# The input projection of an attention layer as three f32r products, with weight slices read from device memory and the split work placed anew

## What is computed

```
def _L0_cond_ref(x, mask, Wq, Wo):        # NH = 8 heads, dk = 64
    xt = jnp.transpose(x, (0, 2, 1))
    q = xt @ Wq.T
    qh = q.reshape(B, T, NH, dk).transpose(0, 2, 1, 3)
    scores = scale * jnp.einsum('bhqd,bhkd->bhqk', qh, qh)
    logits = (scores * cmask + (1.0 - cmask) * NEG) * rmask
    attn = jax.nn.softmax(logits, axis=-1)
    ctx = jnp.einsum('bhqk,bhkd->bhqd', attn, qh)
    ctx = ctx.transpose(0, 2, 1, 3).reshape(B, T, D)
    out = ctx @ Wo.T
    return jnp.transpose(out, (0, 2, 1))

x = x + _L0_cond_ref(x, cond_2048, L0_cond_Wq, L0_cond_Wo)
x = x + _L1_cond_ref(x, cond_2048[:, None, :], L1_cond_b)   # causal conv over 16 sequences, plus a bias
```

## Time and profile before

| | |
|---|---|
| median of 3 runs | 4114.28 us (4113.2 to 4120.28) |
| the profiled execution | 4113.86 us |
| its span | 4112.1 us |
| mean granted TensorE clock | 0.99 |
| TensorE busy | 3982.2 us, 97% of the span |
| ScalarE, GpSimd, VectorE busy | 2768.7, 2683.2 and 2395.2 us |
| loads and stores of device memory | 44 GB/s over the span |

### The profile page before, as it was taken

How to read it: one execution, slowest core, us unless ns; L and a number is a source line. 1 busy time by engine, 2 the same in 40 slices (tenths; PEclk the granted TensorE clock), 3 DMA queues, 4 the chain that set the end, 5 groups by cost and what they waited for, 6 DMA issues and landing times. The chain is left out here.

```text
span 4112.1 us, 58673 instructions
## 1 busy us (share of the span) xinstructions
PE 3982.2 (97%) x19200; PEld 2608.8 (63%) x19200; DVE 2395.2 (58%) x2263; ACT 2768.7 (67%) x3848; POOL 2683.2 (65%) x1105
## 2 busy tenths in 40 slices
PE   7999999999999999999999999999999999999799
PEld 4666666666666666665666666666666666666598
DVE  4665555556465555656555565656556555656676
ACT  4775767667576766757676675767667676767465
POOL 4775767767576776757676675767668576767200
PEclk8999999999999999999999999999999999999899
DMA  4433444343444434344343434434443443443587
GB/s 113 103 93 88 100 106 113 92 109 88 97 102 95 118 93 103 93 97 102 91 118 94 103 93 103 104 88 113 98 106 85 103 107 90 110 103 71 159 291 264
DMA packets 308556, 452.16 MB, mean 110 GB/s; under 512 B 155043, under 2 KB 223267, under 8 KB 308134
## 3 DMA queue, kind: packets, MB, share of 16 engines
q1 hardware_dynamic: 308262, 448.18, 43.5%
HBM read 112.28 MB, written 67.11 MB: 44 GB/s over the span
## 5 line engine op out<-in xcount | busy, mean ns | idle before, releaser
L759 POOL TENSOR_TENSOR plo<-p,phi 128x1024 fp32r<-128x1024 f32 x1024 | 2535.8, 2486 | 1146.8 <-ACT phi L675 1143.5
L810 DVE TENSOR_REDUCE mrow<-misc 128x1 f32<-128x1024 f32 x1024 | 1200.9, 1214 | 826.2 <-PE misc L502 826.0
L673 ACT ACTIVATE p<-sc 128x512 f32<-128x512 f32 x2048 | 1108.6, 593 | 753.8 <-PE sc L544 616.6
L675 ACT ACTIVATE phi<-p 128x1024 fp32r<-128x1024 f32 x1024 | 1086.2, 1061 | 32.6
L543 PE MATMUL sc<-quer,keys 128*128 128x512 f32 x2048 | 879.7, 430 | 21.3 <-issue 17.8
L556 PE MATMUL pv<-phi,val 128*96 128x512 f32 x2048 | 850.9, 415 | 18.0 <-issue 18.0
L544 PE MATMUL sc<-quer,keys 96*128 96x512 f32 x2048 | 811.8, 396 | 0.0
L558 PE MATMUL pv<-phi,val 128*64 128x512 f32 x2048 | 808.9, 395 | 0.0
L562 PE MATMUL pv<-plo,val 128*96 128x512 f32 x2048 | 641.8, 395 | 0.9 <-POOL plo L759 0.9
L556 PEld LDWEIGHTS pv<-phi,val 128*96 128x96 f32 x2048 | 332.3, 162 | 335.4 <-issue 172.2
L543 PEld LDWEIGHTS sc<-quer,keys 128*128 128x128 f32 x2048 | 387.8, 189 | 169.5 <-issue 57.8
(11 more groups left out here) (80 smaller groups left out, 3480.4 us busy)
## 6 DMA issues: line engine op xcount, KB each, us to landing
keys<-hi SPq DMA_DIRECT2D x256, 256.0 KB, 3.1
quer<-mhi SPq DMA_DIRECT2D x256, 256.0 KB, 4.9
keys<-lo SPq DMA_DIRECT2D x128, 256.0 KB, 5.9
quer<-mlo SPq DMA_DIRECT2D x128, 256.0 KB, 3.8
xo<-x SPq DMA_DIRECT2D x64, 512.0 KB, 4.3
x<-xo SPq DMA_DIRECT2D x64, 512.0 KB, 4.8
xin<-x SPq DMA_DIRECT2D x16, 2048.0 KB, 13.8
out<-stage SPq DMA_DIRECT2D x64, 512.0 KB, 6.3
```

What stands on the lines that cost most here:

```text
L673: act.activation(p32[:, t % NP32, half(h)], sc[:, h, :], ACT.Exp, scale=SCALE).then_inc(s_p32, 1)
L675: act.activation(phi[:, t % NPHI, :], p32[:, t % NP32, :], ACT.Copy).then_inc(s_phi, 1)
L759: pool.tensor_tensor(plo[:, t % NPLO, :], p32[:, t % NP32, :], phi[:, t % NPHI, :].bitcast(F32), ALU.subtract).then_inc(s_plo, 1)
L810: reduced = dve.tensor_reduce(mrow[:, q:q + 1], misc[:, k, :], AX.X, ALU.max)
```

## The change

The input projection becomes three f32r products as well. x and both weights are split into a high part rounded to f32r and the remainder: xh and xl, wqh and wql, woh and wol. The weights are split once, at the start, stored to device memory (`keep`), and read back in slices of 512 KB: one for each pair (`wqs`, `load_wq`), one for each quarter of the output (`wos`, `load_wo`). x is loaded to `x32` in four parts at pair 2, head 0, behind the transfer of the row of maxima; ScalarE makes xh of it and VectorE and GpSimd two parts of xl each, in head 1 of pair 2. `mlo` gives up its buffer and is made in `lo`, once `lo` has been moved. The tables of maxima, stages, reciprocals, normalisation and of the split of the context are new.

```diff
+HI_AT = {0: 0, 2: 1, 3: 2, 4: 3}
+LO_POOL = {3: 1, 6: 3}
+LO_DVE = {1: [0], 5: [2]}
-MAX_AT = {0: [0, 1], 1: [2, 3], 3: [4, 5], 4: [6, 7]}
+MAX_AT = {0: [0, 1], 2: [2, 3], 3: [4, 5], 4: [6, 7]}
-REC_AT = {(0, 5): [0], (0, 6): [1], (0, 7): [2], (1, 0): [3], (1, 1): [4], (1, 2): [5], (1, 3): [6], (1, 4): [7]}
-NORM_AT = (1, 5)
+REC_AT = {(0, 5): [0, 1], (0, 6): [2, 3], (0, 7): [4, 5], (1, 5): [6], (1, 6): [7]}
+NORM_AT = (1, 7)
-STAGE_AT = {2: ["mhi", "lo"], 3: ["mlo"]}
-HIGH_AT = (1, 7)
-LOW_AT = (1, 7)
+STAGE_AT = {2: ["mhi"], 3: ["lo"], 6: ["mlo"]}
+HIGH_AT = (0, 0)
+LOW_AT = (0, 0)
...
@@ block.sync
+                if not (isinstance(b, int) and b == 0 and p == 0):
+                    if isinstance(b, int) and b == B - 1 and p == PAIRS - 1:
+                        sp.dma_start(wqs[:].bitcast(F32), wo_kept[2].rearrange("w p k e -> p w k e")).then_inc(s_wqs, 16)
+                    else:
+                        load_wq((p + 1) % PAIRS)
...
+            def keep(t, n, kept, done):
+                sp.wait_ge(done, n)
+                sp.dma_start(kept.rearrange("m p k e -> p k m e"),
+                             t.bitcast(F32).rearrange("p k (m e) -> p k m e", e=P)).then_inc(s_kept, 16)
...
             def store_xo(b, m, more=0):
                 sp.wait_ge(s_xo, b * 2 * DT + 2 * m + 2 + more)
+                if more:
+                    load_wo(3, 0)
+                elif not (isinstance(b, int) and b == B - 1):
+                    load_wo((m + 2) % DT, m % 2)
...
                 operands(0, 0)
+                keep(wqh, 2, wq_kept[:, 0], s_wqh)
+                keep(wql, 2, wq_kept[:, 1], s_wql)
+                keep(woh, 1, wo_kept[:, 0], s_wo_high)
+                keep(wol, 1, wo_kept[:, 1], s_wol)
                 operands2(0, 0, 0, None)
+                sp.wait_ge(s_kept, 64)
+                load_wq(1)
+                for m in range(2):
+                    load_wo(m, m)
                 sp.wait_ge(s_zero, 3)
                 rows(0, 0, 0)
...
                         if phase != "last" and (p, i) == (2, 1):
-                            load_x(b + 1, pair(b, 3) + 1)
+                            load_mask(b + 1, pair(b, 3) + 1)
...
                             rows(nb, np_, ni)
+                        if phase != "last" and (p, i) == (2, 0):
+                            for k in range(DT):
+                                load_x(b + 1, k)
...
@@ block.tensor
-                for k in range(DT):
-                    last = pe.matmul(out, wq[:, k, np_ * P:(np_ + 1) * P], xb[:, k, half(h)],
-                                     start=(k == 0), stop=(k == DT - 1))
+                elif h == 0:
+                    pe.wait_ge(s_wqs, 16 * pair(nb, np_))
+                if phase != "start" and h == 0 and np_ == 0:
+                    pe.wait_ge(s_xl, split_done(nb, 2, 2))
+                    pe.wait_ge(s_xl_pool, 2 * nb)
+                for n, (w, xs) in enumerate(((0, xh), (1, xh), (0, xl))):
+                    for k in range(DT):
+                        last = pe.matmul(out, wqs[:, w, k, :], xs[:, k, half(h)],
+                                         start=(n == 0 and k == 0), stop=(n == 2 and k == DT - 1))
...
@@ block.scalar
+            def input_high(b, k):
+                act.wait_ge(s_xk[k], 16 * b)
+                act.activation(xh[:, k, :], x32[:, k, :], ACT.Copy).then_inc(s_xh, 1)
...
+                            if phase != "last" and (p, i) == (2, 1) and t in HI_AT:
+                                input_high(b + 1, HI_AT[t])
-                            if (i, t) == HIGH_AT and not (phase == "first" and p == 0):
-                                context_high(*before(b, p))
+                            if (i, t) == HIGH_AT and not (phase == "first" and p < 2):
+                                context_high(*before(*before(b, p)))
...
@@ block.gpsimd
+            def input_low(b, k):
+                pool.wait_ge(s_xh, split_done(b, DT, k + 1))
+                pool.tensor_tensor(xl[:, k, :], x32[:, k, :], xh[:, k, :].bitcast(F32), ALU.subtract).then_inc(s_xl_pool, 1)
...
@@ block.vector
                     dve.wait_ge(s_lo, pair(b, p) + 1)
-                    dve.tensor_tensor(mlo[:], lo[:].bitcast(F32), mask[:], ALU.mult).then_inc(s_masked, 1)
+                    for i in range(2):
+                        dve.wait_ge(s_kq[i], 64 * (pair(b, p) + 1))
+                    dve.tensor_tensor(lo[:], lo[:].bitcast(F32), mask[:], ALU.mult).then_inc(s_masked, 1)
...
+            def input_low(b, k):
+                dve.wait_ge(s_xh, split_done(b, DT, k + 1))
+                dve.tensor_tensor(xl[:, k, :], x32[:, k, :], xh[:, k, :].bitcast(F32), ALU.subtract).then_inc(s_xl, 1)
```

More of the change, by code:

```diff
@@ L373, in operands2 @@
                 move(keys2[0:DK, i, :], hi, i).then_inc(s_kq2[i], 16)
[L374 removed]
+                move(quer2[0:DK, i, :], lo, i).then_inc(s_kq2[i], 16)
             def context_rows(b, p, i):
@@ L525, in out_project @@
                     pe.wait_ge(s_ctl, PAIRS * (prev_b + 1))
-                cols = slice(m * P, (m + 1) * P)
-                for n, (w, c) in enumerate(((woh, cth), (wol, cth), (woh, ctl))):
+                ws = wqs if phase == "end" and m == 2 else wos[:, 0 if phase == "end" and m == 3 else m % 2]
+                if phase == "end" and m == 2 and h == 0:
+                    pe.wait_ge(s_wqs, 16 * PAIRS * B)
+                elif phase == "end" and m == 3 and h == 0:
+                    pe.wait_ge(s_wos[0], 16 * (2 * B))
+                elif h == 0:
+                    pe.wait_ge(s_wos[m % 2], 32 * prev_b + 16 * (m // 2) + 16)
+                for n, (w, c) in enumerate(((0, cth), (1, cth), (0, ctl))):
                     for k in range(PAIRS):
-                        last = pe.matmul(out, w[:, k, cols], c[:, k, half(h)],
+                        last = pe.matmul(out, ws[:, w, k, :], c[:, k, half(h)],
                                          start=(n == 0 and k == 0), stop=(n == 2 and k == PAIRS - 1))
@@ L775, in batch, with end @@
                             split(b, p, i, t, phase == "first" and p == 0 and i == 0)
-                            if (i, t) == LOW_AT and not (phase == "first" and p == 0):
-                                context_low(*before(b, p))
-            run(pool, start, batch, lambda: None)
+                            if phase != "last" and (p, i) == (2, 1) and t in LO_POOL:
+                                input_low(b + 1, LO_POOL[t])
+                            if (i, t) == LOW_AT and not (phase == "first" and p < 2):
+                                context_low(*before(*before(b, p)))
+            def end():
+                context_low(B - 1, PAIRS - 2)
+            run(pool, start, batch, end)
         @block.vector
@@ L880, in start @@
                 table_masks()
-                for parts in STAGE_AT.values():
-                    for part in parts:
-                        stage(0, 0, part)
+                dve.wait_ge(s_wqh, 1)
+                dve.tensor_tensor(wqs[:, 1], wq32[:, :, 0:P], wqs[:, 0].bitcast(F32), ALU.subtract).then_inc(s_wql, 1)
+                first_low(0)
+                first_low(1)
+                stage(0, 0, "mhi")
+                stage(0, 0, "lo")
+                weights_low()
+                stage(0, 0, "mlo")
                 do("start", 0, 0, "head", PHASES["start"]["head"], (0, 0, 0))
-                weights_low()
             def batch(phase, b):
@@ L900, in batch @@
                                     normalise(*before(b, p))
+                            if phase != "last" and (p, i) == (2, 1):
+                                for k in LO_DVE.get(t, []):
+                                    input_low(b + 1, k)
             def table_masks():
```

98 lines of the change are left out of this document (68 added, 30 removed).

## The result

| | before | after |
|---|---|---|
| median of 4 runs each, us | 4113.74 (4111.21 to 4120.28) | 4085.43 (4082.28 to 4090.08) |
| the profiled execution's span | 4112.1 | 4083.8 |
| mean granted TensorE clock | 0.990 | 0.988 |

The ratio is 0.9928, with a 95% interval of 0.9916 to 0.994: the change makes the kernel 28 us faster. 4132 was forecast, and slower was given 0.57.

The account below looks back on a forecast made before the run. TensorE, 97% busy, was taken as the bound. From 4113.9 us: -79 - 18 + 22 + 50 + 22 + 6 + 15 = +18, so 4132 us; own range 4120 to 4146, whole range 4070 to 4176.

Parts of the forecast that it names:

- lo and mlo: Pairs other than pair 2: late mlo delays the next head's maxima, costing 0.75 us twice a batch, +22 us.
- Only their cost moves: Head 0: moving two tiles of maxima from step 1 to step 2 only moves their cost, no saving.
- x remainders: Pair 2, head 1: GpSimd's load makes TensorE wait before pair 3's first projection; +3.35 us a batch, +50 us.
- rival B: Remainders of x cost TensorE nothing, waiting under 0.5 us at pair 3's first projection; 4082 us, chance 0.25.
- SP: Pair 1: SP's queue of transfers brings head 1's row of maxima late, +0.4 us a batch, +6 us.
- the projection: Input projection: twelve f32r matmuls take 2.80 us where four fp32 took 3.43, over 126 halves, -79 us.
- the cover of the copy: Step 2 of head 1: maxima cover the wait for ScalarE's copy, 2.91 us becomes 2.33, -18 us.
- pair 1: Output halves wait for banks of maxima (1.16, 0.8, 1.0 us), an old wait of 1.42 goes; +22 us.
- the start: First scores come at 52 to 60 us for 42.5, behind splits, stores and slices of weights; +14 us.
- `lo` comes first in the loop: Head 0, other pairs than pair 2: `lo` starts before the next plo, so step 5 has its maxima in time.
- rival A: `lo` comes second, behind plo; the maxima's transposition waits 1.15 us in three pairs a batch; 4172 us, chance 0.22.
- Rival C: No change to measure: mlo's lateness is absorbed and 22 us go; 4110 us, chance 0.14.

Follow-up runs that it names:

- the first experiment: The kernel before with only the table of maxima changed, two tiles moved from step 1 to step 2: 4332.96 us, ratio 1.053.
- both gains together: The changed kernel with output halves moved off the maxima and the first row of maxima sent before the wait for stored weights: 4037.78 us, ratio 0.982.

## Why the prediction was wrong

The direction was missed through terms of waiting that were too high, two of which were wholly absent, and through a saving in head 0 that the forecast put at nothing.

- **The step that failed: "lo and mlo", +22.** The forecast had mlo "behind a plo until 19" and, from this, the next head's maxima 3.5 us late. In the trace mlo waits 0.63 for the landing of `lo`, a microsecond earlier than reckoned (the moves land in 5.1 us, not 5.9), starts when the running plo is almost over, and takes 1.45. Over the run it takes 1.59 in the median, and over 3 us once in 64 pairs. The maxima of the next head are 0.86 late (1012.87, where 0.54 behind their matmuls at 1011.47 were due), which the steps take up: step 2 is 3.16 us. Measured: 0. mlo made twice shows the mechanism itself at work once VectorE is some 3 us later. The error was to put the worst turn at the lock (a whole plo) on every operation that might meet one.
- **Head 0, missed in "Only their cost moves".** From the scores of step 0 to those of step 3 it is now 14.38 us in pair 0 (981.97 to 996.35). In pair 2, averaged over the loop, these three steps are 1.62 us shorter than before, where the projection alone was to give 1.26: 0.36 more in each of four pairs, some 20 us over the loop. Most of it is a wait that the forecast kept "now as before": the maxima behind the projection wait until ScalarE has read the bank. TensorE's weight loads for them show it between 700 and 3200 us, before and after:

```profile
PEld misc L502 <- ACTq L633: 17.6, 42, 0.4
```

```profile
PEld misc L567 <- ACTq L701: 7.9, 43, 0.2
```

That is 0.42 us a pair, then 0.18. The table of maxima alone decides it: put into the kernel before it gives 7.2 us in total in 40 waits, and taken back in the changed kernel 17.6 in 41; steps 1 and 2 of head 0 become 0.23 shorter and 0.25 longer by it.
- **x remainders, +50: right mechanism, too large.** TensorE waits 1.49 for xl. Averaged over the loop, step 2 of pair 2, head 1 is 3.82 us, 0.7 more than a plain step with maxima, and steps 6 and 7 are 0.27 and 0.49 longer than before. Net it is 2.8 us a batch against 3.35, so +42. Doing the remainders twice confirms that GpSimd's work decides; rival B, its condition a wait under 0.5, was wrong, though its number (4082) was the nearest.
- **SP, +6:** no wait for the row of maxima of pair 1 shows. 0.
- **Right:** the projection (-79: 2.77 us a half against 2.80), the cover of the copy (2.91 + a step of 3.15 became 2.32 + 3.16), pair 1 (waits of 1.03, 0.71 and 1.09 in the profile; taking them away gave 43 us), and the start (+12.1 against +14; the slices are issued at 45.62 as reckoned; below).
- **Right by luck:** that `lo` comes first in the loop. By the prediction's figures it was 0.03 us late, and by its own rows 0.08 (it adds 2.27 where 1051.55 to 1053.77 are 2.22), yet it was taken to be first. In the trace `lo` starts at 1000.29 and the plo beside it at 1000.34. With a shorter projection (two products in place of three) it is late in most pairs.

Timeline of SyncE's issues at the start, of after (beside the earlier trace rows):

```profile
28.19 0.68 SPq L433 DMA_DIRECT2D wq_kept<-wqh  x1
...
45.62 0.38 SPq L437 DMA_DIRECT2D wqs<-wq_kept  x1
```

Sum of the corrections: -22 - 20 - 8 - 6 = -56, and 4132 - 56 = 4076. Of the 9 us that are left to the median of 4085 the timeline names the place. Outside of the loop, in all four pairs of batch 0 and two of batch 15, `mhi` loses its turn and takes over 3 us (last section), and TensorE then waits at step 4. Pair 0 of batch 0, after:

```profile
76.23 0.50 PE L567 MATMUL misc<-quer 64*128 64x512 f32 x2 [0.87 <-DVE mrow L906]
```

In these six pairs steps 4 and 5 of head 0 are together 9.4 us longer than before. The forecast had feared this of `lo`, as rival A. Small differences at the start and in pair 1, of 2 to 3 us each, stay below what this sum can resolve. Rival C named the very thing, that mlo's lateness is absorbed, with 0.14, but its number (4110) was 25 us off; B had nearly the number and not the mechanism. A forecast from four guessed waits, each taken at its expected worst, is no forecast of their sum.

## What to carry to other kernels

An operation of VectorE that shares the lock with GpSimd costs its own time, or a whole plo more. Directly behind another such operation, with a plo pending, it cost a plo more in each case shown here: space them. Behind a reduction it depends on which of the two starts first, by hundredths of a microsecond, so read the durations again after each edit that shifts either engine. Take tables that place work on several engines as one edit; half of one was worth +219 and +122 us here. And before giving work to an engine with a low share of busy time, look at the stretch: in the changed kernel VectorE is busy for 59% and GpSimd for 71%, and more work on either where x is split cost 54 and 82 us.

## What the runs showed of the hardware

**Turns at the lock.** An operation that comes while the other engine's one is running gets the turn right after it (mlo 1.45, 2.67). One that stands directly behind its like, with a plo pending, loses the turn and takes 3.3 to 3.4 us in place of 1.2 (`lo` 3.43 in the first experiment, the second mlo 3.31, ca 3.38). By the Trainium skill (SBUF — State Buffer, Who interferes with whom) the shared ports are an exclusive lock; these durations agree. And who comes first can hang on very little: mlo of the first experiment stands behind reductions and takes 3.42, since a plo starts 0.02 us ahead of it. `mhi` in batch 0 of the changed kernel, outside of the loop:

```profile
71.67 3.38 DVE L892 TENSOR_TENSOR mhi<-hi,mask 128x1024 fp32r<-128x1024 f32 x1
```

GpSimd there, and in batch 4:

```profile
71.55 9.11 POOL L843 TENSOR_TENSOR plo<-p,phi 128x1024 fp32r<-128x1024 f32 x3 [1.46 <-ACT phi L743]
```

```profile
996.95 17.34 POOL L843 TENSOR_TENSOR plo<-p,phi 128x1024 fp32r<-128x1024 f32 x6 [2.37 <-ACT phi L743]
```

In batch 0 the plo starts 0.12 ahead of `mhi` (71.55 and 71.67); in batch 4 `mhi` starts at 996.90, 0.05 ahead of the plo, and takes 1.22. Batch 4 stands 0.05 us from the slow side: rows of another kernel, read to 0.1 us, could not have called this race, and the changed kernel wins it in every pair of its loop.

**The clock as a price of waiting.** A wait of TensorE of about 2 us or more was often followed by a stretch at 1.2 GHz (0.51 and 0.54 in the windows above). In the 14 batches of the loop such a stretch came behind all 42 waits at step 4 of the maxima alone (2.7 us in the rows above) and all 14 of the longest waits with four remainders on VectorE (4.1 us) and with GpSimd's done twice (3.4), but behind only 7 of the 14 waits of 2 us with the splits earlier. Mean granted clocks: 0.988 and 0.989 where such waits are rare (after, both gains together), 0.977 to 0.983 in the three versions that make TensorE wait around the splits of x, 0.978 with the old maxima, and 0.963 with the maxima alone. So a wait of 2 us can cost nearly 4 (2 of standing, and 1.7 of the 3.5 at the lower clock). In after, the waits of 1 us in pair 1 and those of 1.5 for xl had no such stretch; it came in 3 of the 14 batches, each time at the start of the batch, where TensorE stands for some 1.5 us (1.8 at most). No experiment varied the clock by itself: that part is read from the rows, not shown.
